# Sums of squares in halves of 32 tokens on 64x32 tiles of TensorE, in a fused delta-rule attention and FFN kernel on one core

## What is computed

```python
q = _short_conv(hidden_states @ Wq.T, conv_q)   # 4 taps, then silu; k and v alike
q = _l2norm(q); k = _l2norm(k)                  # x * rsqrt(sum(x * x, -1) + 1e-06)
A = where(tri_strict, -(kb @ k.T), 0); T = inverse(eye - A)
u = T @ v; w = T @ kb
# over the chunks: u_adj = u_i - w_i @ S; o_i = q_i @ S + attn @ u_adj; S += k_i.T @ u_adj
```

## Time and profile before

| what | value |
|---|---|
| runs of the kernel | 707.66, 708.82, 711.4 us (median 708.82) |
| the profiled execution's own time | 703.88 us |
| its span | 701.9 us |
| PE, matmuls | 572.8 us, 82% of the span, 7980 matmuls |
| PE, weight loads | 458.1 us, 65% |
| DVE | 486.5 us, 69% |
| POOL | 410.4 us, 58% |
| ACT | 282.6 us, 40% |
| mean granted TensorE clock | 0.913 of full speed |

### The profile page before, as it was taken

One profiled execution on the slowest core, in us unless ns is written; L12 is line 12 of the kernel. 1 busy time (PEld: TensorE's weight loads), 2 busy tenths in 40 slices (PEclk: granted clock), 3 DMA queues, 4 the chain that ended last, 5 costly groups with the idle time before them and its releaser, 6 DMA issues.

```text
span 701.9 us, 20321 instructions
## 1 busy us (share of the span) xinstructions
PE 572.8 (82%) x7980; PEld 458.1 (65%) x7980; DVE 486.5 (69%) x1166; ACT 282.6 (40%) x703; POOL 410.4 (58%) x503
## 2 busy tenths in 40 slices
PE   3788858997877686879898989989976777999964
PEld 2466645665655565667787867878865566888853
DVE  6899675565464543388879878797865566888864
ACT  2588851113444333244454443443513323444421
POOL 4411006784100698279998458998459999666532
PEclk9899989999999676799999999999979898999997
DMA  8629333990124222731304323122250111422201
GB/s 265 181 66 267 122 118 100 244 231 7 34 61 50 43 61 61 75 74 29 75 13 107 80 42 89 47 44 77 61 88 20 35 47 39 87 61 54 56 15 30
DMA packets 112941, 57.15 MB, mean 81 GB/s; under 512 B 82256, under 2 KB 104656, under 8 KB 112848
## 3 DMA queue, kind: packets, MB, share of 16 engines
q1 hardware_dynamic: 112848, 55.87, 34.7%
HBM read 36.89 MB, written 18.95 MB: 80 GB/s over the span
## 4 chain that ended last, share of the span: by engine, by line
DVE 27%; POOL 25%; PE 24%; issue 13%; DMA 4%; SPq 4%; ACT 2%; POOLq 0%; DVEq 0%; ACTq 0%
POOL seq L576 7%; PE bank L1544 6%; DVE arena L1163 6%; POOL seq L574 6%; POOL arena L585 5%; DVE cva L1045 4%; PE bank L1732 4%; DVE arena L1260 3%; PE bank L1614 3%; PE bank L1648 2%; POOL arena L547 2%; SPq L370 2%; DVE seq L1298 2%; PE bank L1625 2%; PE bank L1457 2%
## 5 line engine op out<-in xcount | busy, mean ns | idle before, releaser
L1163 DVE SCALAR_TENSOR_TENSOR arena<-bank,small,arena 128x256 f32<-128x256 f32 x192 | 91.6, 482 | 28.2 <-ACT arena L819 23.4
L585 POOL TENSOR_TENSOR arena<-arena,neg_half 128x2 f32<-128x2 f32 (+1 forms) x64 | 61.7, 964 | 71.6 <-DVE arena L1255 51.1
L576 POOL TENSOR_TENSOR seq<-seq 128x31 f32<-128x31 f32 (+15 forms) x124 | 86.5, 698 | 9.7
L574 POOL TENSOR_TENSOR seq<-seq 128x31 f32<-128x31 f32 (+15 forms) x124 | 69.6, 561 | 7.9
L1137 DVE TENSOR_TENSOR seq<-bank,seq 128x384 f32<-128x384 f32 x64 | 35.3, 557 | 29.7 <-PE bank L1544 19.3
L1544 PE MATMUL bank<-arena 128*64 128x192 f32 x512 | 51.4, 345 | 4.7 <-DVE seq L1137 3.7
L819 ACT ACTIVATE arena<-bank,small 128x256 f32<-128x256 f32 x64 | 30.4, 475 | 61.7 <-PE bank L1614 61.6
L505 POOL TENSOR_TENSOR seq<-seq 128x256 f32<-128x256 f32 x32 | 23.3, 729 | 54.3 <-DVE seq L1137 54.2
L531 POOL TENSOR_TENSOR arena<-seq,powers 128x16 f32<-128x16 f32 x16 | 47.3, 2955 | 10.9 <-DVE seq L1172 10.9
L1614 PE MATMUL bank<-arena,w_k 128*128 128x268 f32 x128 | 43.3, 482 | 6.5 <-DMA arena<-xnT_scratch 5.1
L1614 PE MATMUL bank<-arena,w_q 128*128 128x268 f32 x128 | 36.3, 417 | 13.7 <-DVE arena L1163 13.6
(11 more groups left out here) (159 smaller groups left out, 1434.3 us busy)
## 6 DMA issues: line engine op xcount, KB each, us to landing
arena<-fl SPq DMA_DIRECT2D x32, 192.0 KB, 5.8
arena<-fms SPq DMA_DIRECT2D x32, 192.0 KB, 6.1
arena<-xnT_scratch SPq DMA_DIRECT2D x32, 134.0 KB, 2.8
gram_scratch<-arena SPq DMA_DIRECT2D x16, 256.0 KB, 2.3
arena<-v_scratch SPq DMA_DIRECT2D x32, 128.0 KB, 3.1
arena<-x SPq DMA_DIRECT2D x64, 64.0 KB
out<-arena SPq DMA_DIRECT2D x64, 64.0 KB, 2.1
xnT_scratch<-seq SPq DMA_DIRECT2D x2, 1027.0 KB, 6.2
```

What stands on the lines that cost most here:

```text
L574: pool.tensor_tensor(part, below, above, ALU.mult).then_inc(s["solve"], 1)
L576: last = pool.tensor_tensor(into, into, part, ALU.add)
L585: pool.tensor_tensor(dst, src, half8 if k == U else neg_half[:, 0:k], ALU.pow).then_inc(s[dst_sem], 1)
L1163: nc.vector.scalar_tensor_tensor(cv[:, t], ps[:, :, j:j + C], conv_w[:, 1 - t // 2, t % 2, j:j + 1], cv[:, t], ALU.mult, ALU.add).then_inc ...
```

## The change

The tokens of a unit are taken in two halves of 32. The weights of one matmul are then 64 channels by 32 tokens, and the four matmuls of a unit go to four column groups of the array in turn: tokens 0 to 31 of the first head, of the second, then tokens 32 to 63 of the first, of the second. There are 64 matmuls in the source for a chunk's sums in place of 32. POOL's first halo copy gets a wait for `banks_ready`.

```diff
@@ halo(n), GpSimd
                 pool.wait_ge(s["xf"], 2 * n)
+                if n == 0:
+                    pool.wait_ge(s["banks_ready"], 1)
                 pool.tensor_copy(xf[:, :, :, 0:1], xf[:, :, :, C:C + 1]).then_inc(s["halo"], 1)
@@ sumsq(m, kind), TensorE
                 for u in range(U):
-                    for q in HH:
-                        last = mm(bank[1][q, NONE * (U * kind + u):NONE * (U * kind + u) + NONE], sq[q, U * kind + u], ones[q],
-                                  start=True, stop=True)
+                    for t in (slice(0, HALF), slice(HALF, C)):
+                        for q in HH:
+                            last = mm(bank[1][q.start + t.start:q.start + t.stop, NONE * (U * kind + u):NONE * (U * kind + u) + NONE],
+                                      sq[q, U * kind + u, t], ones[q], start=True, stop=True)
                 last.then_inc(s["sumsq_" + "kq"[kind]], 1)
```

## The result

The changed kernel takes 715.43 us (median of 20 runs), the kernel before 709.86 (20 runs on the same chips): a ratio of 1.0083, 95% interval 1.0049 to 1.0117. The forecast was 704.9 with a range of 700 to 712; time and sign were both wrong. All ratios here leave disturbed executions out on both sides, so that a ratio can differ from the quotient of two medians.

The account below looks back on a forecast made before the run. PE's queue was taken to bound lead steps 0 to 3, mostly DVE and POOL the chunk steps; -1.4 - 1.5 - 1.0 + 0.02 = -3.9 us from the 708.82 median gave 704.9 us, range 700 to 712.

Parts of the forecast that it names:

- The pace: Bursts of sums: four tiles work side by side, 8 ns a record; a chunk takes 1.02 us in place of 1.86.
- The rival of 16 ns: Bursts of sums: only two tiles work at a time, 16 ns a record; +1.9 us, so 710.7; chance 0.20.
- the 25 ns of the page of the Trainium skill: Bursts of sums: the skill's floor from matmul start to start; burst 3.2 us, sum +8.6, so 717; no separate chance.
- The slower rival: Bursts of sums: each load and matmul pair costs 29 ns whatever its width; burst 3.7 us, so 725; chance 0.10.
- Chunk steps: Behind the sums PE is 0.75 us earlier: worth 0 in six steps, -1.5 us in two where DVE waited.
- Gain 0.1 for PE, none for DVE: Usual chunk step, k projection: PE gains 0.1 us until it waits for DVE's L1172; worth 0 in six steps.
- The two chunk steps that were to give 1.5 us: Two later chunk steps where DVE waited for `ffn_v`: it comes 0.75 us earlier, worth 0.72 and 0.75.
- Lead steps, -0.36 each: Lead steps of chunks 0 to 3: second Gram half starts 0.36 us earlier, four times, -1.4 us in all.
- The gap at record 64 for the square of q1: Lead steps: PE waits before the second half of the sums for ACT's square of q1, losing half the gain.
- The clock, -1.0: Falls to the low clock after the sums in lead steps 0 and 2: a third of 3.0 us saved.
- The halo wait: POOL's first halo copy: one added, already satisfied wait, about 0.02 us.
- the sum of -3.9 us: Whole kernel: lead steps -1.4, chunk steps -1.5, clock -1.0, halo wait +0.02 us.

Follow-up runs that it names:

- e1: The changed kernel with 96 more instructions (192 satisfied semaphore waits) at the head of TensorE's program: 711.95 us, ratio 1.0016 to the kernel before.
- e5: The changed kernel with 28 extra small matmuls (112 instructions) at the head of TensorE's program: 710.63 us, ratio 1.0058 to the kernel before.
- e10: The changed kernel with halves only in the chunk steps, lead steps as in the kernel before: 715.88 us, ratio 1.0084 to the kernel before.
- e9: The changed kernel with halves only in the lead steps, chunk steps with the 64x64 tiles of the kernel before: 708.66 us, ratio 1.0032.
- e14: Repeat of the changed kernel with only q's sums in halves and 48 small matmuls at the head: 704.25 us, 0.9931; kernel before with those matmuls: 0.9953.
- e11: The changed kernel with only the sums of q in halves and 48 small matmuls at TensorE's head: 706.41 us, ratio 0.9965 to the kernel before.

## Why the prediction was wrong

- **The pace: right.** 8 ns a record was forecast; 9 ns were measured (0.96 us for 109 starts), 2048 records busy for 24.7 us where I expected 20. Four tiles do work side by side. The rival of 16 ns and the 25 ns of the page of the Trainium skill, from start to start, are both out: the records show 9.
- **The missing term.** No step of the sum priced the bringing in of instructions. I took the doubled time at the low clock as proof that "the array works it off, not the instruction stream"; that was true of the pace and said nothing of the supply. The slower rival named the right place, "the front of PE's queue, which now has 256 instructions per chunk to bring in where it had 128", and gave it the wrong form: a price for each record, from which it followed that 8 ns would rule it out. The price is a lump at every 256th instruction, and the faster the records, the larger the lump. It had 0.10 in my chances.
- **Chunk steps: right in gain, wrong in loss.** "Gain 0.1 for PE, none for DVE" held: in e1 and e5 the k projection waits for L1174. But that cover works one way. The burst with its gap is 0.85 us longer than before, and as PE and VectorE had been level, the k projection came 1.0 us later in the mean of steps 1 to 6. The six steps priced at 0 and two at a gain lost, in e10 alone, 7.6 us between the medians, though not evenly.
- **The two chunk steps that were to give 1.5 us** gave nothing in the kernel after; VectorE waits 9.5 us in six places for `ffn_v` where it waited 4.8 in five.
- **Lead steps, -0.36 each: right where no gap falls.** In lead step 2 the second Gram half starts 1.48 us behind the first record of the burst, against 1.85 in the earlier trace rows. The gap at record 64 for the square of q1 is there. But three bursts and one Gram half met an edge, the store of chunk 3's Gram matrices was issued at 216.6 us and not before 215 (before: 215.74), and e9, with the lead part alone, shows no gain.
- **The clock, -1.0:** it gave nothing. The low clock behind the burst of lead step 0 did not come (the Gram half took 1.09 us there, not 1.81), but in lead step 1 it came behind the gap of 2.18 us (granted clock 0.50 from 188 to 190 us, Gram half 1.97), and lead step 2 kept it (1.97). The mean granted clock was 0.907 against 0.913 before. **The halo wait** was left in all variants of the kernel after and not tried alone; in the trace GpSimd goes into that copy, at 301.5 us, with no idle time ahead of it, and e14 has the wait at a ratio of 0.9931.

The step that failed is thus the missing term: the bringing in of TensorE's instructions, put at nothing, stands in the trace with 17.6 us of idle time inside the bursts. Whether the sum of -3.9 us would have come out without it is not shown: e1 and e5, without gaps in the chunk steps, are not faster than the kernel before, and the gain of e11 and e14 is not separated from their control.

## What to carry to other kernels

Count instructions, not only time: where a change makes the same work out of more and faster instructions, see how long the engine takes for any 256 in a row, and compare it with the 2.4 to 3.5 us that a block needed to arrive here (it came later still in some lead steps). The mark of it is idle time put down to "issue" in the middle of a loop without waits, at a position that moves by a fixed count from step to step. And where two engines are level at a join, price a gain at nothing and a loss at up to its full size.

## What was not expected of the hardware

- TensorE's instructions come in blocks of 256; a stream of fast ones is held to 3.46 us a block where its records need 1.7 us, and in this kernel a crossing that comes too soon stops the engine for 0.9 to 3.5 us. So in that stream the mean is 3.46 us / 128 = 27 ns for each pair of load and matmul, though within a block they start 13 ns apart (9 ns in the kernel, at the full clock).
- 16 instructions at the head of a program of some 18,500 moved the gaps of all eight chunk steps by 8 records: where the edges fall is a property of the whole program ahead of them, and 96 instructions far away took all eight gaps out.
- In the lead steps some packets started up to 10 us and more behind the crossing, so that PE stopped at the end of blocks that had lasted about 12 us; the reason stays open.
